# A decoder layer with a routed feed-forward network: three sorted groups of 2, 3 and 2 batches instead of four of 1, 2, 2 and 2

## The chip, the cores and the metric

The kernel runs on one core of a Trainium2 chip. The metric is the device time of one execution in microseconds (us). A core has a matrix engine (PE; its weight loads are listed as PEld), a vector engine (DVE), a scalar engine (ACT), a general engine (POOL), and a queue, SP, that does no arithmetic here and starts most of the transfers. Each engine takes its instructions in the order in which they are written, and waits at a semaphore until another engine or a transfer has raised it.

## The reference

The input `x` has 8 batches of 256 tokens of width 128. Three blocks follow one another, each with a residual and a layer norm: attention with selected keys, retention against a context, and a feed-forward network with 8 experts, of which each token takes the two with the highest gate. The last one is what the change touches:

```
logits = x_flat @ gate_w.T;  probs = softmax(logits)
topk_probs, topk_idx = top_k(probs, 2)
hidden = relu(einsum('th,ehf->tef', x_flat, w1) + b1)      # 8 experts, 128 -> 512
all_out = einsum('tef,efh->teh', hidden, w2) + b2          # 512 -> 128
y = sum(take_along_axis(all_out, topk_idx) * topk_probs)
x = layernorm(x + y)
```

The reference works out all experts for all tokens. The kernel does so for the last batch alone; for the other seven it sorts tokens by expert.

## The kernel before

**Steps and slots.** The whole kernel is one pipeline, written by the function `program` that every engine walks through. Step n (n from -2 to 8) has 20 slots. In slot s of step n, each engine gets its instructions of four stages: attention's preparation for batch n+1 (stage a), attention's 16 query tiles of batch n (stage b, one in each of slots 0 to 15), retention and the second norm of batch n-1 (stage c), and the router (stage d), whose gates and counts for batch n-1 stand in slots 16 to 19. Step 7 has no stage a, step 8 neither a nor b.

**Sorted groups.** Batches 0 to 6 are taken in groups (`GROUPS`). A group's tokens, each twice, once for each chosen expert, are laid out in DRAM so that each stretch of 128 rows belongs to one expert. Since the number of tokens of an expert is known only at run time, a group of b batches needs as many tiles as the worst case: `most_tiles` = (2·256·b + 8·127) // 128, which is 11 for one batch, 15 for two and 19 for three. All of them are computed, empty or not. A group goes through this:

- `tile_list(g)`, in slot 2 of the step that is two behind its last batch. DVE works out each token's row (`slot`) and each tile's expert (`lrow`), in a chain of small operations with four for each batch. POOL then scatters the tokens of each batch with four indirect transfers (L780). SP waits for `lrow`, starts the weights of three tiles, waits for the scatter, and loads the first rows.
- `tile(g, k, q)`: the tiles, one in each tile slot of the plan. In tile k's slot PE does the second product of tile k (L1202), the turning of tile k+2's rows, and the first product of tile k+1 (L1185); ACT does four rectifications (L1467), DVE two copies out of PSUM (L1855, L1862). Two slots (k = -2 and -1) start a group and one (k = number of tiles) only stores. SP starts the expert weights of tile k+3 (578 KB), the rows of tile k+4 and the store of tile k-1. Up to the last group, `tile` shares the bank `bR` with retention and router; in the last group (`g == ALONE`), which runs in step 8, it uses the banks that attention has left.
- For each batch: `collect` (G; POOL gathers its rows with four indirect transfers, L768), `summed` (S; POOL, three operations), `means` (M; DVE and ACT, statistics) and `normed` (N; root on DVE, normalising on POOL in L808, and SP, which waits for POOL and stores the batch, L628). The last group's and batch 7's stand behind the last slot, with batch 7's eight experts (`dense`).

**The plan.** `plan` fills the free tile slots in order: in steps 2 to 7 the nine `TILE_SLOTS`, in step 8 the 22 `END_SLOTS`. A group begins in slot 6 or later of the step of its list. This is what it gives before, T for tiles computed:

```
step 2: list of batch 0 in slot 2; 3 tiles of group 0 (slots 13, 15, 17)
step 3: 8 tiles of group 0; G0 in slot 19
step 4: S0, M0, N0 (slots 0, 7, 8); list of 1, 2; 3 tiles of group 1
step 5: 9 tiles of group 1
step 6: 3 tiles of group 1 (0, 1, 2); list of 3, 4; G1 S1 G2 S2 M1 N1 M2; 3 tiles of group 2
step 7: N2 in slot 0; 9 tiles of group 2
step 8: 3 tiles of group 2; list of 5, 6; G3 S3 G4 M3 S4 N3 M4 N4 in slots 5 to 18; 15 tiles of group 3
behind: batch 7 with all 8 experts; G S M N of batches 5 and 6
```

## Time and profile before

| | |
|---|---|
| median of 3 runs | 766.42 us (762.03 to 773.82) |
| the profiled execution | 757.35 us, of which its span is 755.5 us |
| PE busy | 644.0 us, 85% of the span |
| DVE busy | 473.1 us, 63% |
| ACT busy | 369.5 us, 49% |
| POOL busy | 274.7 us, 36% |
| granted clock of PE, mean | 0.868 of full |
| weights `wt` | 64 loads of 578 KB, median 4.1 us from issue to landing |

How to read it: busy time is the sum of an engine's instructions, and a busy PE can still be slower than it might be, since its clock changes between half and full. The span is shown in 40 slices, with the clock in each. What a step costs is read from windows: a step begins here where ACT's first exponential of that batch begins (51.5, 114.4, 180.7, 253.9, 326.6, 407.0, 481.6 and 562.1 us for steps 0 to 7), and step 8 where PE starts the tile of its slot 0 (639.5 us).

### The profile page before, as it was taken

What the parts mean: (1) busy time and instruction counts of PE and PEld (TensorE: products, weight loads), DVE (VectorE), ACT (ScalarE), POOL (GpSimd) and SP (SyncE); (2) the same over time, 40 slices, a digit from 0 to 9 for tenths busy, and PEclk for the clock granted to TensorE, in tenths of its full rate; (3) what the DMA queues carried; (4) which work ended last, traced back from release to release, by engine and by line L of the source; (5) the groups of instructions that cost most, each with busy time, mean ns of one, the idle gap of its engine ahead of it and who ended that gap; (6) DMA issues with size and microseconds to landing.
All of it is one profiled execution on the core that took longest, in us unless ns stands there. A gap on an engine that the chain in (4) does not pass through costs nothing.

```text
span 755.5 us, 18822 instructions
## 1 busy us (share of the span) xinstructions
PE 644.0 (85%) x6549; PEld 495.8 (66%) x6549; DVE 473.1 (63%) x1733; ACT 369.5 (49%) x1271; POOL 274.7 (36%) x451
## 2 busy tenths in 40 slices
PE   5469988997999899988998999889977997567794
PEld 4245664675577677755686777757766776457794
DVE  1618647876985797578766975687744674314334
ACT  4335445453565476544554766355533643234352
POOL 0345602911840163139701540179622001342053
PEclk9857598897799999965899999968986998669998
DMA  4080030020306330303044416040523222248760
GB/s 150 1 299 2 2 106 1 2 107 1 124 3 204 108 97 19 111 16 129 9 170 127 116 41 195 23 144 17 172 86 101 87 82 64 87 138 267 227 214 26
DMA packets 43413, 73.23 MB, mean 97 GB/s; under 512 B 7664, under 2 KB 31544, under 8 KB 42168
## 3 DMA queue, kind: packets, MB, share of 16 engines
q1 hardware_dynamic: 41528, 68.36, 28.7%
q0 software_dynamic: 1792, 3.67, 1.5%
q8 instruction: 53, 0.87, 0.5%
q14 instruction: 40, 0.33, 0.1%
HBM read 61.69 MB, written 10.32 MB: 95 GB/s over the span
## 4 chain that ended last, share of the span: by engine, by line
PE 44%; issue 10%; POOL 9%; DVE 8%; ACT 3%; DMA 1%; POOLq 0%; DVEq 0%
PE bM L830 6%; PE bG L975 5%; PE bH L1185 5%; PE bR L1202 4%; PE bM L1018 3%; PE bS L994 3%; PE bM L1023 2%; POOL sorted_tokens L780 2%; PE bR L1107 2%; PE bW L1247 2%; PE bS L991 2%; PE bC L830 2%; PE bC L1124 2%; PE bW L1202 1%; PE bC L1075 1%
## 5 line engine op out<-in xcount | busy, mean ns | idle before, releaser
L1385 ACT ACTIVATE pp<-pp,nmx 128x224 f32<-128x224 f32 x96 | 46.4, 483 | 79.5 <-DVE nmx L1662 78.1
L1668 DVE TENSOR_TENSOR gs<-bG,rank_t 96x512 f32<-96x512 f32 x96 | 65.5, 682 | 18.5 <-PE bG L975 18.5
L1467 ACT ACTIVATE ht<-bH,wt 128x128 f32<-128x128 f32 x192 | 54.7, 369 | 39.1 <-PE bH L1185 39.1
L1397 ACT COPY pts<-bM 128x256 f32<-128x256 f32 x96 | 35.4, 369 | 63.0 <-PE bM L830 62.7
L1731 DVE TENSOR_TENSOR sm<-bC,cst 128x512 f32<-128x512 f32 x64 | 43.6, 681 | 34.0 <-PE bC L1124 33.6
L1202 PE MATMUL bR<-wt,ht 128*128 128x128 f32 x328 | 51.1, 305 | 15.8 <-DVE taken L1808 13.3
L726 POOL TENSOR_TENSOR r<-x,cst 128x256 f32<-128x256 f32 x8 | 5.8, 724 | 153.7 <-DVE x L1695 153.7
L975 PE MATMUL bG<-oh,kspl 128*96 128x512 f32 x160 | 61.3, 467 | 0.0
L1202 PEld LDWEIGHTS bR<-wt,ht 128*128 128x128 f32 x328 | 46.9, 215 | 21.2 <-issue 15.1
L1185 PE MATMUL bH<-xt,wt 128*128 128x128 f32 x384 | 56.6, 295 | 4.1 <-DVE xt L1855 2.0
L1650 DVE TENSOR_SCALAR ppn<-pp,rls 128x224 f32<-128x224 f32 (+1 forms) x128 | 49.8, 389 | 14.1 <-DVE rls L1647 0.5
L830 PE MATMUL bM<-cst,ppn 128*128 128x128 f32 (+1 forms) x224 | 56.2, 323 | 0.9 <-DVE ppn L1650 0.9
L1185 PEld LDWEIGHTS bH<-xt,wt 128*128 128x128 f32 x384 | 52.5, 210 | 5.8 <-DVE xt L1855 2.7
L1662 DVE CUSTOM_DVE_ANT_0 pp<-bS,cst 128x224 f32<-128x224 f32 x96 | 36.5, 380 | 29.1 <-PE bS L994 29.1
L1018 PE MATMUL bM<-pts,ckw 96*32 96x64 f32 x512 | 52.6, 293 | 0.3 <-ACT ots L1405 0.3
L1124 PE MATMUL bC<-qV,kS 128*128 128x512 f32 x64 | 37.0, 578 | 13.1 <-DVE sm L1731 10.6
L994 PE MATMUL bS<-gs,qall 96*32 96x128 f32 x768 | 44.7, 308 | 1.0 <-DVE gs L1668 0.2
L780 POOL DMA_INDIRECT sorted_tokens<-x,slot x28 | 29.9, 1068 | 42.7 <-DVE slot L1837 27.5
L1018 PEld LDWEIGHTS bM<-pts,ckw 96*32 96x32 f32 x512 | 19.5, 113 | 39.2 <-issue 38.3
L1023 PEld LDWEIGHTS bM<-pts,vgs 128*32 128x32 f32 x1536 | 44.2, 121 | 0.0
L830 PE MATMUL bM<-cst,gs 32*128 32x32 f32 x384 | 44.0, 236 | 0.0
L1023 PE MATMUL bM<-pts,vgs 128*32 128x16 f32 x1536 | 43.4, 198 | 0.0
(288 smaller groups left out, 1595.9 us busy)
## 6 DMA issues: line engine op xcount, KB each, us to landing
wt<-in_experts SPq DMA_DIRECT2D x64, 578.0 KB, 4.1
sidx<-far_slots SPq DMA_DIRECT2D x8, 1536.0 KB, 7.0
xs<-sorted_tokens SPq DMA_DIRECT2D x56, 64.0 KB, 3.7
expert_rows<-ot SPq DMA_DIRECT2D x56, 64.0 KB, 3.5
sorted_tokens<-acc SPq DMA_DIRECT2D x11, 256.0 KB, 7.8
cst<-shape_constants SPq DMA_DIRECT2D x1, 1603.5 KB, 6.3
xn<-in_x SPq DMA_DIRECT2D x8, 128.0 KB, 4.9
xr<-in_x SPq DMA_DIRECT2D x8, 128.0 KB, 3.2
```

Source lines behind the costliest of these rows:

```text
L830: return MM(dst, src, ident[lo:lo + n, lo:lo + n], is_transpose=True, start=True, stop=True)
L975: last = MM(w[0:96, :], table, oh[:, pair % 2, kt, SLOTS * (tile % 2):SLOTS * (tile % 2) + SLOTS], start=(n == 0), stop=(n == len(products ...
L994: last = MM(bS[32 * c:32 * c + 32, o + 96:o + SW], qall[0:96, p, 128 * tile + 32 * c:128 * tile + 32 * c + 32], gs[:, g % 2, 128 * c:128 * ...
L1018: last = MM(bM[32 * j:32 * j + 32, WEIGHED:WEIGHED + 64], near, pts[0:96, 0:128].rearrange("p (q a b) -> p b a q", a=4, b=2)[:, j, :, :], ...
L1023: last = MM(bM[32 * j:32 * j + 32, WEIGHED:WEIGHED + 64].rearrange("p (a q) -> p a q", a=4)[:, :, 4 * c:4 * c + 4], vgs[:, g % 2, 32 * c:3 ...
L1124: full(MM(w[:, :], kS[:, t, g, :], qV[:, g, :, :], start=True, stop=True))
L1185: last = MM(w[:, 128 * f:128 * f + 128], wt[:, t % NW, 128 * f:128 * f + 128], xt[:, t % 2, :], start=True, stop=True)
L1202: last = MM(w[:, 0:128], ht[:, t % 2, f, :], wt[:, t % NW, W2_AT + 128 * f:W2_AT + 128 * f + 128], start=(f == 0), stop=(f == 3))
L1385: AC(pp[:, s % 2, 0:w], bS[:, 0:w] if s < T0 else pp[:, s % 2, :], ACT.Exp, scale=1.0 if s < T0 else -1.0, bias=nmx[:, s % 2:s % 2 + 1], a ...
L1467: last = AC(ht[:, t % 2, f, :], w[:, 128 * f:128 * f + 128], ACT.Relu, bias=wt[:, t % NW, FF + f:FF + f + 1])
L1650: TS(ppn[:, t % 2, 0:w], pp[:, t % 2, 0:w], rls[:, t % 2:t % 2 + 1], None, ALU.mult).then_inc(s_nrm.sem, 1)
L1668: TT(gs[:, g % 2, :].rearrange("p (t j) -> p t j", j=FAR), bG[0:96, :].rearrange("p (t j) -> p t j", j=FAR), rank_t[:, :].rearrange("p (o ...
```

## The change

The groups are (0, 1), (2, 3, 4) and (5, 6), with 15, 19 and 15 tiles: 49 instead of 56. There are three lists instead of four. Steps 6 and 7 get eleven tile slots instead of nine (`FULL_SLOTS`), and step 2 none. `plan` puts sums, statistics and normalising at other distances behind the last tile: in step 8 three slots apart for each batch instead of four, and five slots behind the gather instead of eight. Since three batches wait for their list at a time, `hm` and `place` hold three batches (`PART_OF`); `tile_row` and `row_start` are stored once and broadcast. The new plan:

```
step 2: no tile, no list
step 3: list of 0, 1 in slot 2; 3 tiles of group 0 (slots 13, 15, 17)
step 4: 9 tiles of group 0
step 5: 3 tiles of group 0 (0, 2, 4); G0 7, S0 10, G1 11, M0 12, N0 13, S1 14
step 6: list of 2, 3, 4 in slot 2; M1 4, N1 5; 5 tiles of group 1 (10, 11, 13, 15, 17)
step 7: 11 tiles of group 1 (0, 2, 4, 5, 8, 9, 10, 11, 13, 15, 17)
step 8: 3 tiles of group 1; list of 5, 6; G2 5, G3 8, S2 8, M2 10, G4 11, S3 11, N2 11,
        M3 13, N3 14, S4 14, M4 16, N4 17; 15 tiles of group 2
```

```diff
-GROUPS = tuple((b, most_tiles(b)) for b in ((0,), (1, 2), (3, 4), (5, 6)))
+GROUPS = tuple((b, most_tiles(b)) for b in ((0, 1), (2, 3, 4), (5, 6)))
 DENSE = NB - 1
+PART_OF = [n - next(b for b, _ in GROUPS if n in b)[0] for n in range(DENSE)] + [2]
-ALONE = 3
+ALONE = 2
-MOST = 16
+MOST = 20
 TILE_SLOTS = (0, 2, 4, 5, 8, 10, 13, 15, 17)
+FULL_SLOTS = (0, 2, 4, 5, 8, 9, 10, 11, 13, 15, 17)
 LIST_SLOT, FIRST_SLOT = 2, 6
-MEAN_LATE = 8
...
-    at, free = {}, [(step, s) for step in range(2, NB) for s in TILE_SLOTS] + [(NB, s) for s in END_SLOTS]
+    at, free = {}, [(step, s) for step in range(3, NB) for s in (TILE_SLOTS if step < 6 else FULL_SLOTS)] + [(NB, s) for s in END_SLOTS]
...
-            s += 2 + 4 * (n - GROUPS[g][0][0])
-            for table, late in ((gather, 0), (first, 3), (second, MEAN_LATE), (third, MEAN_LATE + 1)):
-                table[step + (s + late) // NS, (s + late) % NS] = n
+            s += 2 + (4 if step < NB else 3) * (n - GROUPS[g][0][0])
+            mean = NS * step + s + 5
+            if step < NB and not 4 <= mean % NS < 16:
+                mean += 8
+            for table, here in ((gather, NS * step + s), (first, NS * step + s + 3), (second, mean), (third, mean + 1)):
+                table[here // NS, here % NS] = n
...
-        hm, hot = sb("hm", [128, 2, 2, 2, NE]), sb("hot", [128, 2, NE], BF16)
+        hm, hot = sb("hm", [128, 3, 2, 2, NE]), sb("hot", [128, 2, NE], BF16)
-        taken, place = sb("taken", [128, NE]), sb("place", [128, 2, 2, NE])
+        taken, place = sb("taken", [128, NE]), sb("place", [128, 3, 2, NE])
```

The two places that the prediction speaks of, as the instructions stand in order. First SP in step 8, in the last group's tiles: `wt` are a tile's weights, `xs` its rows, `expert_rows` the store of a tile, `out` that of a whole batch, and `lrow` the reading of four tiles' expert numbers. Before, from the weights of tile 10 on:

```order
L581 DMA wt<-in_experts 128x1156
L572 DMA xs<-sorted_tokens3 128x128
L595 DMA expert_rows3<-ot 128x128
L581 ISA
L581 DMA wt<-in_experts 128x1156
L572 DMA xs<-sorted_tokens3 128x128
L595 DMA expert_rows3<-ot 128x128
L628 DMA out<-acc 128x2x128
L194 TENSOR_LOAD lrow
L194 ISA x8
L581 ISA
```

In the change, from the weights of tile 7 on (four lines further down in the file):

```order
L585 DMA wt<-in_experts 128x1156
L576 DMA xs<-sorted_tokens2 128x128
L599 DMA expert_rows2<-ot 128x128
L632 DMA out<-acc 128x2x128
L198 TENSOR_LOAD lrow
L198 ISA x8
L585 ISA
L585 DMA wt<-in_experts 128x1156
L576 DMA xs<-sorted_tokens2 128x128
L599 DMA expert_rows2<-ot 128x128
```

The first store of a batch in the last group's tiles stood between the weights of tiles 11 and 12, and now stands between those of tiles 7 and 8; a second one stands where the first was.

Then PE in step 7, in slots 8 to 10: L991/L995 to L975/L979 are attention's scores and gather, L1202/L1206 and L1185/L1189 a tile's two products, the others attention's transposes and weighing. Before, from slot 8's tile on:

```order
L1202 MATMUL bR<-wt,ht 128x128 x4
L830 MATMUL bR<-cst,xs 128x128
L1018 MATMUL bM<-pts,ckw 32x64 x2
L1023 MATMUL bM<-pts,vgs 32x4x4 x8
L830 MATMUL bM<-cst,gs 128x32 x4
L830 MATMUL bM<-cst,ppn 128x128 x2
L1124 MATMUL bC<-qV,kS 128x512
L1185 MATMUL bH<-xt,wt 128x128 x4
L991 MATMUL bS<-kd,qall 128x96
L994 MATMUL bS<-gs,qall 32x128 x4
L975 MATMUL bG<-oh,kspl 96x512 x2
L1018 MATMUL bM<-pts,ckw 32x64 x2
```

In the change:

```order
L1206 MATMUL bR<-wt,ht 128x128 x4
L834 MATMUL bR<-cst,xs 128x128
L1022 MATMUL bM<-pts,ckw 32x64 x2
L1027 MATMUL bM<-pts,vgs 32x4x4 x8
L834 MATMUL bM<-cst,gs 128x32 x4
L834 MATMUL bM<-cst,ppn 128x128 x2
L1128 MATMUL bC<-qV,kS 128x512
L1189 MATMUL bH<-xt,wt 128x128 x4
L995 MATMUL bS<-kd,qall 128x96
L998 MATMUL bS<-gs,qall 32x128 x4
L979 MATMUL bG<-oh,kspl 96x512 x2
L1206 MATMUL bR<-wt,ht 128x128 x4
```

In slot 9, where attention went on with L1018 directly, a second product (and behind it the rest of a tile) has come in; the same holds for slot 11.

## Rows read from the trace of the kernel before

**Rows 1.** Windows, steps 1 to 8: us; busy PE, PEld, DVE, ACT, POOL; clock; DMA; GB/s.

```profile
114.40:180.70 66.30, 58.40 (x670) 41.30 (x670) 50.92 (x181) 35.39 (x124) 24.95 (x45) 0.90 0.09 32
180.70:253.90 73.20, 65.92 (x724) 48.66 (x724) 54.85 (x199) 39.09 (x140) 27.31 (x49) 0.88 0.31 99
253.90:326.60 72.70, 70.15 (x804) 55.44 (x804) 53.40 (x195) 43.08 (x152) 26.22 (x49) 0.96 0.25 75
326.60:407.00 80.40, 70.71 (x724) 51.69 (x724) 58.30 (x211) 40.14 (x141) 37.19 (x58) 0.80 0.29 95
407.00:481.60 74.60, 70.24 (x824) 55.69 (x824) 54.06 (x199) 45.29 (x159) 22.32 (x45) 1.00 0.34 104
481.60:562.10 80.50, 72.81 (x769) 56.06 (x770) 59.40 (x220) 41.18 (x148) 47.81 (x68) 0.86 0.31 99
562.10:639.50 77.40, 67.44 (x756) 53.81 (x754) 44.35 (x152) 35.03 (x132) 8.08 (x15) 0.87 0.28 81
639.50:755.50 116.00, 83.28 (x579) 74.31 (x579) 40.48 (x161) 40.84 (x125) 41.76 (x48) 0.84 0.50 156
```

**Rows 2.** Windows: slots 7 to 14 of steps 1 and 5, slots 15 to 19 of step 1.

```profile
142.70:168.90 26.20, 24.95 (x357) 17.82 (x357) 20.93 (x69) 14.48 (x49) 10.23 (x19) 1.00 0.22 78
436.40:466.60 30.20, 30.18 (x396) 23.98 (x395) 21.23 (x75) 17.96 (x62) 7.39 (x17) 1.00 0.39 125
168.90:180.70 11.80, 9.01 (x117) 7.60 (x109) 6.97 (x34) 4.74 (x17) 0.44 (x1) 1.00 0.01 2
```

**Rows 3.** Windows: slots 0 to 3 of steps 7 and 5.

```profile
562.10:581.10 19.00, 13.23 (x69) 10.60 (x68) 8.88 (x27) 7.15 (x28) 7.01 (x10) 0.59 0.35 98
407.00:423.00 16.00, 14.60 (x115) 10.93 (x116) 13.28 (x44) 11.99 (x46) 1.99 (x4) 1.00 0.32 91
```

**Rows 4.** Timeline of PE: one tile in step 3 (start us, us, engine, line).

```profile
269.15 1.05 PE L1202 MATMUL bR<-wt,ht 128*128 128x128 f32 x8
...
270.24 0.41 PE L1018 MATMUL bM<-pts,ckw 96*32 96x64 f32 x4
...
271.09 1.06 PE L1185 MATMUL bH<-xt,wt 128*128 128x128 f32 x8
271.90 0.48 PE L1124 MATMUL bC<-qV,kS 128*128 128x512 f32 x1
```

**Rows 5.** Timeline of DVE: first and last operation of the list in step 4.

```profile
334.15 0.18 DVE L1818 TENSOR_TENSOR flag<-taken,cst 128x32 f32<-128x32 f32 x1
...
337.33 0.16 DVE L1845 TENSOR_SCALAR lrow<-owner 1x16 int32<-1x16 f32 x1
```

**Rows 6.** Timeline of POOL: step 6's scatter, first and last of eight.

```profile
492.58 1.09 POOL L780 DMA_INDIRECT sorted_tokens<-x,slot  x1 [8.90 <-DVE slot L1837]
...
502.47 0.96 POOL L780 DMA_INDIRECT sorted_tokens<-x,slot  x1 [0.32 <-issue]
```

**Rows 7.** Timeline of POOL in step 8: G3 (first, fourth), S3 (first, last), N3.

```profile
669.57 0.98 POOL L768 DMA_INDIRECT gb<-expert_rows,slot  x1 [6.68 <-DMA expert_rows<-ot]
...
673.37 0.94 POOL L768 DMA_INDIRECT gb<-expert_rows,slot  x1 [0.31 <-issue]
675.93 1.04 POOL L797 TENSOR_TENSOR gb<-gb,v 128x512 f32<-128x512 f32 x1 [1.62 <-DMA gb<-expert_rows,slot]
...
677.86 0.72 POOL L799 TENSOR_TENSOR acc<-acc,x 128x256 f32<-128x256 f32 x1
...
698.65 1.57 POOL L808 TENSOR_SCALAR acc<-acc,fmv,fln 128x128 f32<-128x128 f32 x2 [8.60 <-DVE fln L1688]
```

**Rows 8.** Timeline of SP and PE in step 8: N3's store, weights, first products.

```profile
693.10 1.06 PE L1185 MATMUL bG<-xt,wt 128*128 128x128 f32 x8
...
700.25 0.39 SPq L628 DMA_DIRECT2D out<-acc  x1
702.18 0.34 SPq L581 DMA_DIRECT2D wt<-in_experts  x1
...
706.17 1.75 PE L1185 MATMUL bG<-xt,wt 128*128 128x128 f32 x8 [2.47 <-issue]
```

More of the change, by code:

```diff
@@ L151, in constants @@
     c["before"] = (p[:, None] < p[None, :]) * 1.0
-    c["tile_row"] = np.tile(np.repeat(np.arange(MOST) * 1.0, NE), (128, 1))
+    c["tile_row"] = np.tile(np.arange(MOST) * 1.0, (128, 1))
     c["nothing"] = np.zeros((128, NE))
     for size in sorted({len(b) for b, _ in GROUPS}):
-        c[f"row_start{size}"] = np.tile(np.arange(size * L // 128) * 128.0, (128, NE))
+        c[f"row_start{size}"] = np.tile(np.arange(size * L // 128) * 128.0, (128, 1))
     return c
@@ L1769, in router @@
                 for r in range(2):
-                    k = od.did(TT(hm[:, i.par, r, :, :], C("expert_no").rearrange("p (o e) -> p o e", o=1).broadcast_to([128, 2, NE]),
+                    k = od.did(TT(hm[:, PART_OF[i.n], r, :, :], C("expert_no").rearrange("p (o e) -> p o e", o=1).broadcast_to([128, 2, NE]),
                                   f8[:, :, r:r + 1].broadcast_to([128, 2, NE]), ALU.is_equal))
                 od.wait(k)
-                TT(hot[:, :, :], hm[:, i.par, 0, :, :], hm[:, i.par, 1, :, :], ALU.add).then_inc(r_m.sem, 1)
+                TT(hot[:, :, :], hm[:, PART_OF[i.n], 0, :, :], hm[:, PART_OF[i.n], 1, :, :], ALU.add).then_inc(r_m.sem, 1)
             oe = Own(dve, own_ve)
@@ L1779, in gates @@
                 for r in range(2):
-                    k = oe.did(TT(hm[:, i.par, r, :, :], C("expert_no").rearrange("p (o e) -> p o e", o=1).broadcast_to([128, 2, NE]),
+                    k = oe.did(TT(hm[:, PART_OF[i.n], r, :, :], C("expert_no").rearrange("p (o e) -> p o e", o=1).broadcast_to([128, 2, NE]),
                                   f8[:, :, r:r + 1].broadcast_to([128, 2, NE]), ALU.is_equal))
@@ L1783, in gates @@
                 for t in range(2):
-                    k = oe.did(TS(gg[:, t, :], hm[:, i.par, 0, t, :], v8[:, i.n, t, 0:1], None, ALU.mult))
+                    k = oe.did(TS(gg[:, t, :], hm[:, PART_OF[i.n], 0, t, :], v8[:, i.n, t, 0:1], None, ALU.mult))
                 oe.wait(k)
                 for t in range(2):
-                    last = STT(gg[:, t, :], hm[:, i.par, 1, t, :], v8[:, i.n, t, 1:2], gg[:, t, :], ALU.mult, ALU.add)
+                    last = STT(gg[:, t, :], hm[:, PART_OF[i.n], 1, t, :], v8[:, i.n, t, 1:2], gg[:, t, :], ALU.mult, ALU.add)
                 last.then_inc(r_gate.sem, 1)
@@ L1818, in tile_list @@
                 k = ol.did(TT(each(flag[:, 0:n]), taken[:, :].rearrange("p (e o) -> p e o", o=1).broadcast_to([128, NE, n // NE]),
-                              each(C(f"row_start{len(batches)}")), ALU.is_gt))
+                              C(f"row_start{len(batches)}").rearrange("p (o r) -> p o r", o=1).broadcast_to([128, NE, n // NE]), ALU.is_gt))
                 ol.wait(k)
@@ L1828, in tile_list @@
                     base = row0[:, :].rearrange("p (o e) -> p o e", o=1).broadcast_to([128, 2, NE])
-                    k = os_.did(TT(place[:, b % 2, :, :], place[:, b % 2, :, :], base, ALU.add))
+                    k = os_.did(TT(place[:, PART_OF[b], :, :], place[:, PART_OF[b], :, :], base, ALU.add))
                     os_.wait(k)
                     k = os_.did(TT(qq[:, :, :].rearrange("p (r t) e -> p r (t e)", r=2),
-                                   hm[:, b % 2, :, :, :].rearrange("p r t e -> p r (t e)"),
-                                   place[:, b % 2, :, :].rearrange("p (o t) e -> p o (t e)", o=1).broadcast_to([128, 2, 2 * NE]), ALU.mult))
+                                   hm[:, PART_OF[b], :, :, :].rearrange("p r t e -> p r (t e)"),
+                                   place[:, PART_OF[b], :, :].rearrange("p (o t) e -> p o (t e)", o=1).broadcast_to([128, 2, 2 * NE]), ALU.mult))
                     os_.wait(k)
@@ L1840, in tile_list @@
                 k = ol.did(TT(past[:, :, :], ends_row.broadcast_to([1, MOST, NE]),
-                              C("tile_row", 1).rearrange("p (t e) -> p t e", e=NE), ALU.is_le))
+                              C("tile_row", 1).rearrange("p (t o) -> p t o", o=1).broadcast_to([1, MOST, NE]), ALU.is_le))
                 ol.wait(k)
```

2 lines of the change are left out of this document (1 added, 1 removed).

## The prediction

> **What bounds the kernel now.** I read the busy times first: PE 85%, DVE 63%, so PE is the candidate, but with room. Then windows step by step [rows 1]. Steps with a list cost more than steps with tiles: step 5 with 9 tiles and no list takes 74.6 us, step 4 with 3 tiles, a list of two batches and one combination takes 80.4. Step 1, with neither, takes 66.3. So a tile in a step without a list is cheap, (74.6 − 66.3) / 9 = 0.9 us, and a list is dear. Third, windows inside steps [rows 2]: slots 7 to 14 take 26.2 us in step 1, where PE is busy 24.95, and 30.2 in step 5, where three tiles fall in them and PE is busy 30.18. There PE is full and a tile costs (30.2 − 26.2) / 3 = 1.3 us, since it first fills PE's gaps. Without gaps it would cost what PE gives it: in the timeline the second product and the turning go from 269.15 to 270.24 and the first product from 271.09 to 271.90, 1.9 us together [rows 4]. Seven tiles at that full price are 13.3 us; that is the most that the title of the change can be worth in PE work.
>
> The lists are dear for two reasons. DVE's chain, from 334.15 to 337.49, holds DVE for 3.3 us in a stretch in which it is full of other work [rows 5], and PE goes slower for lack of work: mean clock 0.80 in step 4 against 1.00 in step 5 [rows 1].
>
> **The change, step by step.** I take each new step as a step of the trace that has the same load. Up to 180.7 us nothing changes but some columns of constants, at no cost.
>
> Step 2 loses its list and three tiles and becomes step 1: 66.3 for 73.2, −6.9 (from −8 to −5: the clock of step 1 was 0.90).
>
> Step 3 had 8 tiles and no list, 72.7; it gets a list of two batches and three tiles. That is the load of step 2 (73.2, a list of one) with four more small DVE operations, 0.2 us each by the operations in [rows 5], 0.9 with their waits, so 74.1 at least. Step 4, which also has three tiles and a list of two, took 80.4, but it combined batch 0 as well and ran at a clock of 0.80. I take 75.5, nearer to step 2 since nothing is combined here: +2.8 (+1.4 to +7.7).
>
> Step 4 had 80.4; it gets nine tiles and no list, which is step 5: 74.6, −5.8 (−7.7, if it is step 3, to −5).
>
> Step 5 had 74.6. It keeps three tiles in slots 0 to 4 and loses six. Its slots 0 to 6 stay at 29.4 (407.0 to 436.4); slots 7 to 14 become those of step 1, 26.2, and slots 15 to 19 too, 11.8 [rows 2]: 67.4. It gets the combination of batch 0 and half of that of batch 1; step 4 is 7.2 longer than step 2 through one combination, one more batch in the list and a lower clock, and I give the combination 1.5 of it. 68.9, −5.7 (−7.2 to 0, if it were all 7.2).
>
> Step 6 had 80.5 with 6 tiles, a list of two and most of two combinations. It gets 5 tiles, the list of three and M1, N1. By step 4: 80.4 + 0.9 + two more tiles at 1.3 = 83.9. By step 2: 73.2 + 2 × 0.9 + 2.6 = 77.6. I take 81.5, a little above the middle, since M1 and N1 stand among DVE's busiest slots: +1.0 (−2.9 to +3.4). POOL's scatter becomes longer, 12 indirect transfers for 8. Eight took from 492.58 to 503.43 [rows 6], so four add 5.4 us. Behind them on POOL stands attention's preparation for the next batch, which slots 7 and 10 want. SP waits for the scatter too, but the first tile's rows are wanted only in slot 8. I cost both at nothing because step 6 loses G1, G2, S1 and S2; if that cover is too small, up to 2 us of PE waiting for POOL come on top.
>
> Step 7 had 77.4. Its slots 0 to 3 took 19.0 us at a clock of 0.59, against 16.0 at 1.00 for the same slots of step 5, which even have stage a in them [rows 3]: batch 2's normalising, in slot 0 of step 7, and the statistics before it hold the queues there. They leave, −3.0. Two tiles come, in slots 9 and 11. In step 7 PE has no gaps to fill from slot 7 on, so I take 1.9 each [rows 4], +3.8. Sum +0.8 (−2.5 with 1.3 a tile and 2 us of clock more, to +3.8).
>
> Step 8 has as many tiles as before, but combines three batches for two, and closer together. G2 begins where G3 began, 669.6, as the same store precedes it. Four gathers take 5.0 with their gaps (669.57 to 674.31, and 0.3), the sum 2.65 (675.93 to 678.58) [rows 7]. In POOL's new order: G2 to 674.6, G3 to 679.6, S2 to 682.3. M2 then needs DVE for about 1.2 us, an estimate from five operations of 0.2 and a little more for their width [rows 5]; G4 waits for it: 683.5 to 688.5, S3 to 691.2, N2 1.6 more [rows 7], 692.8. SP waits for exactly that to store batch 2, and behind it in SP's queue stand the expert numbers and the weights of tile 8. In the trace N3's store at 700.25 is followed by weights at 702.18, and the first product that uses them starts at 706.17 after PE had waited 2.47 [rows 8]: 1.93 and 3.99 us. So tile 8's first product can start at 692.8 + 1.9 + 4.0 = 698.7. It starts at 693.10 now [rows 8]. **+5.6**, and nothing else on PE can fill it, because PE takes its instructions in order. The bounds: 0 if the slots before it run late enough by themselves, +10 if the clock falls behind the wait.
>
> Sum: −6.9 + 2.8 − 5.8 − 5.7 + 1.0 + 0.8 + 5.6 = **−8.2 us**. The profiled execution took 757.35 us (span 755.5), so its counterpart should take 749.1. The runs have a median of 766.42 and spread by 11.8; the profiled one lies 9 below the median. I carry the difference over: 766.42 − 8.2 = **758.2**.
>
> Removed POOL and DVE work of the fourth list does not stand in the sum by itself; the step windows have it. The weight loads saved, 7 of 578 KB, cost nothing now, as the share of DMA in steps 3 to 7 is 0.25 to 0.34 [rows 1].
>
> **The clock, row against rule.** Slots 7 to 14 of step 1 have no tile and ran at a clock of 1.00, PE busy 24.95 of 26.2 [rows 2], so I let steps 2 and 5 keep their clock without tiles. The Trainium skill ("TensorE: Matmul & The Clock Gate", section "Why this matters for your kernels") says that gaps between bursts of matmuls drop the clock to half, and taking tiles out widens the gaps. The trace agrees where gaps are wide: 0.59 at the start of step 7, with PE busy 13.23 of 19.0 [rows 3]. By the row the sum is −8.2; by the rule, applied to every tile-free stretch, it would be the second rival's sum.
>
> **Rivals.** A, *PE gives back the full price*: every tile taken out counts 1.9 us, 13.3 together, the list's DVE chain, once less, about 1.7 net of the longer ones, the stall at the start of step 7 3.0, and SP's wait for N2 is hidden since POOL is faster than I think. −18.0: 739.4 in profile, 748.4 as a median. For it: PE is busy 30.18 of 30.2 where tiles are. Against: steps with 8 or 9 more tiles than step 1 are only 6.4 and 8.3 us longer [rows 1].
>
> B, *the clock*, which ends slower: tile-free steps 2 and 5 and the head of step 3 are run at the clock of step 4. Price: the 7.2 us between steps 4 and 2 for each of steps 2 and 5, −8.2 + 14.4 = +6.2, 772.6. It decides when their clock is under about 0.85. For it: steps 2 and 4 with three tiles had 0.88 and 0.80, step 5 with nine 1.00. Against: [rows 2].
>
> C, *SP's queue*, twice: N3 in step 8 blocks tile 12 a second time by as much, with half clock behind both waits, and the scatter of three holds POOL in step 6 (2 us). −8.2 + 5.6 + 2 = −0.6, 765.8. Against: N3 now has its turn after tile 8 as before, so its wait shifts with the tiles.
>
> **Chances.** Forecast 0.50, A 0.26, B 0.10, C 0.14. The range takes in A and the lower bounds of steps 5 and 8 in part, and B's sum: 743 to 772. About 2%, 15.3 us, is what a measurement can tell from no change here. Faster by more than that needs the median under 751.1: A with most of its share, 0.19, and the forecast's low end, with several steps at their lower bounds, 0.08: 0.27. Slower by more needs +15: B and C together, 0.03. Within 2%: 0.70.
>
> **What would show it.** In the changed profile: step 2 near 66 and step 5 near 69 us with clocks over 0.9; step 4 near 74.6; steps 3 and 6 with clocks near 0.8; in step 8 a wait of PE of some 5 us before the first product of tile 8, with SP storing a batch just before; no dear slot 0 in step 7. I am wrong if PE has no such wait (then A), if step 2 or 5 stays at over 72 us (B), or if a second wait of over 4 us stands before tile 12 (C).

## The result, and the profile after

Measured beside each other in 20 runs each, the changed kernel took **770.39 us** (761.42 to 775.53) and the kernel before 761.97 us (760.11 to 773.82). The ratio is 1.0077, 95% interval [1.0046, 1.0107]: slower by 0.8%, which is less than the 2% that the prediction counts as a change, but more than the measurement's own uncertainty. Two later comparisons on other chips gave 1.0035 [0.999, 1.008] and 1.0067 [1.0036, 1.0099]. The forecast was 8.2 us faster, and that is wrong: the median of 770.4 lies in the range of 743 to 772, but on the other side of no change. An execution over 1.5% above the fastest of its kernel in the same set is counted as slow and left out of the ratios; such are the executions behind the trace that the prediction was read from and behind five of those below (on chip B the changed kernel unchanged and the later normalising, on chip D both repairs, on chip E the kernel before and the parted transfers).

The profiled execution took 768.8 us (span 767.0). The windows of its steps 1 to 8 answer to [rows 1]:

```profile
113.20:177.40 64.20, 55.81 (x670) 39.37 (x670) 50.66 (x181) 35.06 (x123) 25.10 (x45) 0.95 0.10 33
177.40:242.70 65.30, 57.36 (x670) 40.54 (x670) 50.95 (x182) 35.19 (x123) 24.79 (x45) 0.92 0.11 32
242.70:319.80 77.10, 68.06 (x724) 50.04 (x724) 55.31 (x204) 39.45 (x139) 32.80 (x53) 0.84 0.30 97
319.80:395.80 76.00, 71.70 (x824) 57.17 (x824) 54.40 (x199) 45.30 (x159) 22.30 (x45) 0.98 0.35 104
395.80:474.90 79.10, 69.54 (x719) 51.77 (x719) 54.42 (x193) 37.11 (x133) 40.38 (x61) 0.84 0.11 36
474.90:563.00 88.10, 72.53 (x750) 53.91 (x750) 59.53 (x219) 41.00 (x147) 38.27 (x59) 0.81 0.32 105
563.00:639.60 76.60, 70.27 (x794) 56.42 (x794) 45.58 (x153) 37.19 (x139) 6.75 (x13) 0.92 0.33 96
639.60:767.00 127.40, 85.28 (x579) 75.67 (x579) 44.81 (x169) 40.83 (x127) 49.57 (x57) 0.83 0.47 145
```

Read the first column against the terms of the sum. Step 2 fell as forecast (65.3 us, 66.3 forecast), steps 3, 4 and 7 are within 2 us. Three steps are far off: step 5 was to take 68.9 us at a high clock and took 79.1 at 0.84; step 6 took 88.1 for 81.5; step 8 grew by 11.4 for 5.6.

**Step 5.** Its slots 0 to 6, 7 to 14 and 15 to 19 were forecast at 29.4, 26.2 and 11.8 us, plus 1.5 for the combinations:

```profile
395.80:422.90 27.10, 24.91 (x260) 18.04 (x260) 23.61 (x84) 18.01 (x68) 12.39 (x23) 1.00 0.03 9
422.90:455.00 32.10, 29.72 (x348) 20.88 (x348) 22.36 (x76) 14.45 (x51) 21.55 (x28) 0.84 0.21 68
455.00:474.90 19.90, 14.92 (x120) 12.84 (x115) 8.45 (x34) 4.65 (x16) 6.44 (x12) 0.61 0.07 20
```

The first part is better than forecast. The miss is in the other two, where the forecast used slots of step 1 that had run at a clock of 1.00: 5.9 us in slots 7 to 14, at 0.84, and 8.1 in slots 15 to 19, at 0.61. The timeline of POOL in the second half of the step:

```profile
453.19 1.64 POOL L812 TENSOR_SCALAR acc<-acc,fmv,fln 128x128 f32<-128x128 f32 x2 [7.74 <-DVE fln L1692]
454.80 0.73 POOL L730 TENSOR_TENSOR r<-cn,cst 128x256 f32<-128x256 f32 x1
...
456.55 0.72 POOL L735 TENSOR_TENSOR rkn<-r 128x256 f32<-128x256 f32 x1
```

and the timeline of PE at the same time:

```profile
455.67 0.44 PE L834 MATMUL bM<-cst,ppn 128*128 128x128 f32 x2
460.10 1.09 PE L834 MATMUL bC<-cst,rks 128*128 128x128 f32 x4 [4.00 <-DVE rks L1572]
```

POOL stood 7.74 us for the normalising of batch 0 (L812), and the rotation of the retention keys (L730 to L735) was queued behind it. DVE makes rks, the rotated keys, from its result, and PE waited 4.00 us for rks. This wait belongs to slots 15 to 19; it says nothing about slots 7 to 14. The order of POOL's queue was changed by the table that puts batch 0's normalising into slot 13, and I had costed only the combination's own work.

**Step 8.** The timeline of SP, with the first store and what follows it, and the second store:

```profile
692.63 0.39 SPq L632 DMA_DIRECT2D out<-acc  x1
694.57 0.34 SPq L585 DMA_DIRECT2D wt<-in_experts  x1
...
706.59 0.39 SPq L632 DMA_DIRECT2D out<-acc  x1
708.52 0.34 SPq L585 DMA_DIRECT2D wt<-in_experts  x1
```

and the timeline of PE, its two longest waits in that stretch:

```profile
698.53 2.05 PE L1189 MATMUL bH<-xt,wt 128*128 128x128 f32 x8 [3.61 <-issue]
...
712.55 2.05 PE L1189 MATMUL bH<-xt,wt 128*128 128x128 f32 x8 [3.44 <-issue]
```

This is the forecast wait, 5.9 us after the store as the sum had it (1.9 + 4.0): tile 8's first product was forecast for 698.7 and started at 698.53 (step 8 begins at 639.6 here and at 639.5 in the trace of the kernel before, so the two can be compared). The second wait stands before tile 12, where the kernel before had one of 2.47 us [rows 8]; it is now 3.44. So one wait is new, and the old one has grown by 1.0. The product after each takes 2.05 us where the one between takes 1.06: the granted clock is 0.50 from 698.5 to 701.5 and 0.52 from 712.5 to 715.5, and 1.00 from 704 to 706.

**Step 6.** The timeline of DVE:

```profile
493.00 0.66 DVE L1735 TENSOR_TENSOR sm<-bC,cst 128x512 f32<-128x512 f32 x1
498.69 0.39 DVE L1666 CUSTOM_DVE_ANT_0 pp<-bS,cst 128x224 f32<-128x224 f32 x1 [5.03 <-remote]
```

and of PE:

```profile
492.69 0.66 PE L998 MATMUL bS<-gs,qall 96*32 96x128 f32 x8
...
495.40 0.77 PE L1128 MATMUL bC<-qV,kS 128*128 128x512 f32 x1
499.15 0.74 PE L995 MATMUL bS<-kd,qall 128*128 128x96 f32 x2 [2.98 <-DVE nmx L1666]
```

DVE waits for the scores that PE wrote in L998. Their recorded end is 493.35, DVE goes on at 498.69, 5.3 us later, and PE waits for DVE in turn. I call this a **late signal**. POOL issues its twelve scatters from 484.4 to 499.9, 0.3 us apart. I count a signal as late where DVE or ACT waits for a matmul and goes on over 1 us after its recorded end. The changed kernel's trace then has seven places or stretches of them (around 260, 444, 494, 661, 677, 689 and 743 us), and the trace of the kernel before has none.

Of what the prediction named as signs: step 2 near 66, step 4 near 74.6 (76.0) and the wait before tile 8 (3.61 us, some 5 forecast) are there. The dear slot 0 of step 7 is gone only in part, since slots 0 to 3 there (563.0 to 579.0) had a clock of 0.72. One sign of the rivals is there as well, step 5 over 72 (B). The sign of C, a second wait of over 4 us before tile 12, is not: it is 3.44.

### The profile page after: what moved, and what is told of

Its sections match the earlier page's. It is cut to its first block and busy times, and to the rows that moved or that the text cites. A ratio compares the mean times of both kernels' runs of the same rounds, so it can differ in the third digit from the quotient of the medians.

```text
span 767.0 us, 18441 instructions
## 1 busy us (share of the span) xinstructions
PE 632.2 (82%) x6430; PEld 482.0 (63%) x6430; DVE 473.4 (62%) x1713; ACT 360.4 (47%) x1243; POOL 278.5 (36%) x451
## 5 line engine op out<-in xcount | busy, mean ns | idle before, releaser
L730 POOL TENSOR_TENSOR r<-x,cst 128x256 f32<-128x256 f32 x8 | 5.8, 726 | 183.5 <-DVE x L1699 183.5
L1471 ACT ACTIVATE ht<-bH,wt 128x128 f32<-128x128 f32 x168 | 48.0, 369 | 49.5 <-PE bH L1189 44.5
L1189 PE MATMUL bH<-xt,wt 128*128 128x128 f32 x336 | 51.3, 301 | 11.4 <-issue 7.8
L979 PE MATMUL bG<-oh,kspl 128*96 128x512 f32 x160 | 59.4, 454 | 0.0
L1189 PEld LDWEIGHTS bH<-xt,wt 128*128 128x128 f32 x336 | 47.3, 214 | 13.2 <-issue 8.2
L1206 PE MATMUL bR<-wt,ht 128*128 128x128 f32 x272 | 41.1, 299 | 13.7 <-DVE taken L1812 11.1
L1206 PEld LDWEIGHTS bR<-wt,ht 128*128 128x128 f32 x272 | 37.1, 207 | 18.8 <-issue 12.4
L995 PE MATMUL bS<-kd,qall 128*128 128x96 f32 x192 | 39.6, 291 | 7.7 <-DVE nmx L1666 7.6
L998 PE MATMUL bS<-gs,qall 96*32 96x128 f32 x768 | 43.9, 303 | 2.4 <-DVE gs L1672 0.2
L1022 PEld LDWEIGHTS bM<-pts,ckw 96*32 96x32 f32 x512 | 19.4, 112 | 40.1 <-issue 39.1
```

Of the source, the lines that this page charges most:

```text
L979: last = MM(w[0:96, :], table, oh[:, pair % 2, kt, SLOTS * (tile % 2):SLOTS * (tile % 2) + SLOTS], start=(n == 0), stop=(n == len(products ...
L998: last = MM(bS[32 * c:32 * c + 32, o + 96:o + SW], qall[0:96, p, 128 * tile + 32 * c:128 * tile + 32 * c + 32], gs[:, g % 2, 128 * c:128 * ...
L1022: last = MM(bM[32 * j:32 * j + 32, WEIGHED:WEIGHED + 64], near, pts[0:96, 0:128].rearrange("p (q a b) -> p b a q", a=4, b=2)[:, j, :, :], ...
L1189: last = MM(w[:, 128 * f:128 * f + 128], wt[:, t % NW, 128 * f:128 * f + 128], xt[:, t % 2, :], start=True, stop=True)
L1206: last = MM(w[:, 0:128], ht[:, t % 2, f, :], wt[:, t % NW, W2_AT + 128 * f:W2_AT + 128 * f + 128], start=(f == 0), stop=(f == 3))
L1471: last = AC(ht[:, t % 2, f, :], w[:, 128 * f:128 * f + 128], ACT.Relu, bias=wt[:, t % NW, FF + f:FF + f + 1])
```

## The experiments

Eighteen runs followed, of fourteen kernels, on five further chips (here B to F; the first comparison is A). Ratios are always against the kernel before, run in turns on the same chip. Each run left one trace, so where the text sets windows of two runs side by side, it compares one execution with one. "Tail" is the time from the last exponential of attention in step 7 to the end: 130.8 us in the first trace of the kernel before, 142.2 in that of the changed kernel.

### Chip B: the changed kernel again, one repair each, and the tiles alone

The changed kernel unchanged:

> The changed kernel once more, nothing edited. Its first profile has six places (at 260, 442, 493, 660, 676 and 741 us) where PE's semaphores rise 1.3 to 5.9 us after the recorded end of the matmul that raises them, with DVE and ACT waiting; the profile of before has none. Theory P (these late signals are a part of the change's cost): they come again at the same places, and the time is again 767 to 772. Rival (an accident of one execution): they stand elsewhere or are gone, and a profile without them has a span near 755 to 760. In either case a PE wait of some 3.5 us before the first product of tile 8 of the last group, and one of some 4 us for the split keys at the end of step 5.

Measured: 1.0035 [0.999, 1.008]. Its trace has no late signal anywhere, so they are no fixed part of the change. Its span is 765.7 all the same and not near 755 to 760: steps 0 to 2 took 210.0 us, 20 more than in the first trace, at clocks of 0.72, 0.79 and 0.82. Step 6 is 80.7 (81.5 forecast) and the tail 136.0, 5.2 more than before (5.6 forecast). Before tile 8 PE waited 4.91, before tile 12 3.53, and in step 5 1.95 for rks. At the place of step 6 shown above, DVE's timeline reads:

```profile
506.83 0.66 DVE L1735 TENSOR_TENSOR sm<-bC,cst 128x512 f32<-128x512 f32 x1
507.42 0.37 DVE L1666 CUSTOM_DVE_ANT_0 pp<-bS,cst 128x224 f32<-128x224 f32 x1
```

No gap, with the same twelve scatters running (498.19 to 514.4). So the scatters alone do not make the signals late; something that differs between chips or executions has to be there too.

Batch 0's normalising two slots later:

```
-            for table, here in (..., (third, mean + 1)):
+            for table, here in (..., (third, mean + (3 if n == 0 else 1))):
```

> The changed kernel with batch 0's normalising moved from slot 13 to slot 15 of step 5, so that on POOL the rotation of retention's keys (slot 14) stands ahead of it and not behind it. Theory W (order in the queues costs what was not foreseen): PE's wait of 4.0 us for the split keys at 460 us goes, step 5 falls from 79 to about 75 us, the time by 4 us. Rival C (the half clock of the tile-free half of step 5 sets its length): the wait goes but step 5 stays within 1.5 us, since what PE does behind it is as slow as before.

Measured: 0.999 [0.9929, 1.0051]; step 5 71.0 us at a clock of 0.93, 3 under the changed kernel beside it. PE's wait for rks is gone. Slots 15 to 19 take 11.8 us at a clock of 1.00, as the prediction had them, while slots 7 to 14 stay at 32.2 at 0.84. The gain in time is not clear of noise.

SP's stores of batches 2 to 4 two slots later in step 8:

```
+STORE_AT = {(step, s + 2 if step == NB else s): n for (step, s), n in NORM_AT.items()}
...
+                    if stored and (step, s) in STORE_AT:
+                        stored(STORE_AT[step, s])
```

> The changed kernel with the stores of batches 2, 3 and 4 issued by SP two slots later in step 8 than they are normalised; POOL, DVE, ACT and PE keep their order. Theory W (SP's queue blocks the weights of tiles 8 and 12): PE's waits of 3.6 and 3.4 us before the first products of these tiles go, and the time falls by 5 to 7 us. Rival: the sums of batch 4, which need batch 2's store to have landed, and through them the statistics come later and hold DVE: no gain, or under 2 us.

Measured: 0.9918 [0.9875, 0.996], 1.2% under the changed kernel; the intervals of the two do not meet. The tail is 125.1. PE's waits for SP's weights in step 8, 4.91 and 3.53 in the changed kernel beside it, are now 0.36, 0.83 and 1.08:

```profile
689.40 1.13 PE L1196 MATMUL bH<-xt,wt 128*128 128x128 f32 x8 [0.36 <-issue]
...
692.36 1.13 PE L1196 MATMUL bG<-xt,wt 128*128 128x128 f32 x8 [0.83 <-issue]
...
697.91 1.13 PE L1196 MATMUL bG<-xt,wt 128*128 128x128 f32 x8 [1.08 <-issue]
```

The kernel before with seven tiles fewer, its groups kept and the slots left empty; the rows of those tiles are left out:

```
+LEFT_OUT = (1, 2, 2, 2)
+GROUPS = tuple((b, most_tiles(b) - m) for b, m in zip(((0,), (1, 2), (3, 4), (5, 6)), LEFT_OUT))
```

> The kernel before with 10, 13, 13 and 13 tiles in its four groups, 49 for 56; the slots of the seven left-out tiles stay empty, and every list, gather, sum and normalising keeps its slot. It leaves out the last one or two tiles of each group. It prices the seven tiles alone. By the forecast's cheap price (0.9 to 1.3 us a tile) the time falls by 6 to 9 us, by the full price (1.9) by 13 us. If PE's clock falls where the tiles are missing, by under 4 us.

Measured: 0.9769 [0.9673, 0.9866], 17 us for seven tiles. By the interval it is 10 to 25 us, so the 13.3 that I had as the most is not ruled out. The tail is 119.7, 11.1 less than in the first trace of the kernel before, and it loses four of the seven tiles. The regrouping takes no tile out of step 8: there are the second products of 19.4 tiles behind the last exponential before and after, 15.4 here.

### Chip C: is it the stores, and what is a tile worth in step 8?

The kernel before with late stores (the same table, bounded to slot 19):

> The kernel before, with SP's stores of the combined batches in step 8 two slots later, nothing else. Theory (SP's queue is dear only where its wait for the normalised batch comes out above the work behind it, and the kernel before had one such wait of 2.47 us, ahead of tile 12): the gain is small, 2 to 4 us, ratio 0.995 to 0.998, and step 8 falls from 116.0 to some 113. The regrouping with the same edit then is ahead of it or level, by 746.5 for the changed kernel with late stores against 752 to 754 here. Rival (late stores help either kernel alike, since what they relieve is the end of the kernel and not the two waits that the regrouping made): ratio 0.99 or below, and the regrouping itself is worth nothing.

Measured: 0.9996 [0.9958, 1.0033]. A gain of the late stores in the kernel before is not to be seen; the interval leaves room for 0.4%. So what they gain on chip B is for the most part a loss that the regrouping had made.

Both repairs:

> The changed kernel with both repairs: batch 0 normalised two slots later in step 5, so that it stands behind the retention's key rotation on POOL, and SP's stores in step 8 two slots later. Theory (two separate losses, one in step 5 and one in step 8): step 5 at 71 or less, step 8 near 110; the late normalising alone measured 0.999 and the late stores 0.992 against the kernel before, the changed kernel 1.0035, so the two together give about 0.988, some 746 us. Rival (the clock takes back in the next steps what step 5 gives): level with late stores alone, 0.992.

Measured: 0.994 [0.9912, 0.9969]; step 5 71.0 at 0.93. Here, too, the signals are late: step 6 87.2, tail 131.4.

Both repairs, and the middle group's 19 tiles ended in step 7:

```
-FULL_SLOTS = (0, 2, 4, 5, 8, 9, 10, 11, 13, 15, 17)
+FULL_SLOTS = (0, 2, 4, 5, 8, 9, 10, 11, 12, 13, 14, 15, 16, 17)
...
+    late = ((2, ((7, 17), (8, 0), (8, 4), (8, 5))), (3, ((8, 3), (8, 6), (8, 8), (8, 9))), ...)
```

> The changed kernel with both repairs and with tiles moved out of step 8: step 7 takes all that is left of the middle group, twelve tiles, and step 8 only the last group's fifteen, with the gathers of batches 2 to 4 a few slots earlier. The number of tiles stays at 49. Theory (a tile is cheap in steps 3 to 7, at most 1.9 us, and costs over 3 us in step 8, where the kernel with seven empty tile slots fewer lost 10.9 us for three tiles): step 8 falls by some 10 us against the one with both repairs, step 7 and 6 grow by 2 to 6 us together, ratio 0.977 to 0.985. Rival (the price in step 8 is the last group's chain from its list to its last gather, which does not get shorter by this): level with both repairs, step 7 longer by what step 8 gives.

Measured: 1.0031 [0.9987, 1.0075], 0.9% behind both repairs. Step 6 grew by 8.7 for three tiles, the tail stayed at 131.5, although four tiles had left it and the last group's rows were loaded some 6 us sooner. In the tail the time went here, in PE's timeline:

```profile
667.56 0.47 PE L847 MATMUL bS<-cst,xs 128*128 128x128 f32 x1 [1.47 <-issue]
676.09 0.79 PE L1141 MATMUL bC<-qV,kS 128*128 128x512 f32 x1 [8.06 <-issue]
```

In these 8 us POOL issued five indirect transfers, gathers of batches 3 and 4, and ACT went on 7.9 us after the recorded end of the matmul that it waited for: a late signal again. The time is level, as the rival had it, but its reason, the chain of the last group, is not what shows. The edit moves the sums and normalisings of batches 2 to 4 too, so it is no test of a tile's place alone.

The kernel before with three tiles fewer in its last group (`GROUPS = GROUPS[:3] + ((GROUPS[3][0], GROUPS[3][1] - 3),)`); their rows are left out:

> The kernel before with twelve tiles instead of fifteen for the last group of two batches; what would have stood in the last three tiles is left out. It gives the price of a tile in step 8 by itself. Theory (3.3 to 3.6 us each there, since in the last step nothing else is left that fills PE while a tile's chain runs): 10 to 11 us less, ratio 0.985 to 0.987. Rival (a tile costs PE's own 1.9 us as elsewhere, and the seven tiles less gained their 17 us otherwise): 4 to 6 us less, ratio 0.992 to 0.995.

Measured: 0.9925 [0.9884, 0.9967], 5.7 us, 1.9 a tile (0.8 to 3.0 by the interval). The rival holds, my 3.3 to 3.6 was wrong; I had counted three tiles for four in the kernel with 49. The price read in [rows 4] fits step 8.

### Chip D: more PE work in the steps without tiles

> The changed kernel with both repairs once more, as the base for the two kernels with added PE work on the same chip. Theory (the two losses are the wait in step 5 and SP's two waits in step 8): 0.99 against the kernel before, as in the first measurement (0.994 [0.991, 0.997]); the same again if the repairs don't depend on the chip.

Measured: 0.9985 [0.9941, 1.003]. That is less of a gain than on chip C (0.994 [0.9912, 0.9969]), but the two intervals overlap, so that the repairs depend on the chip is not shown. In its trace PE's wait for rks is gone, and yet slots 15 to 19 of step 5 take 16.2 us at a clock of 0.50: here the clock fell 7 us before them.

> The changed kernel with the late stores alone once more, beside the one with both repairs. Theory (normalising batch 0 two slots later has a gain of its own, 3 to 6 us in step 5, through a wait of 4 us that goes and the clock behind it): 0.4 to 0.8% behind both repairs. Rival (it has none, step 5's length is the clock's luck): level with both repairs within 0.3%.

Measured: 0.9986 [0.9946, 1.0026], level with both repairs: the rival holds. What the earlier normalising costs is too small for these measurements.

A product without a reader in every slot, or every second one, of the steps without tiles:

```
+                    if fill and step >= 0 and (step < 3 or (step == 5 and s >= 7)):
+                        fill()
...
+            def fill():
+                MM(bH[:, 0:256], ident, wq_all[:, 0:256], start=True, stop=True)
```

> Both repairs, and in every slot of the steps that have no tile (steps 0, 1, 2 and slots 7 to 19 of step 5) one more product on PE, of 128 by 256 elements, whose result nobody reads: 73 products, about 0.3 us each at full clock, 22 us of PE work. Theory (the clock falls in tile-free stretches for lack of PE work, half clock for 12 to 24 us in a step, and more work keeps it up, as the tiles of step 4 did in all traces, 0.98 to 1.00): clocks of steps 0, 1, 2 and 5 over 0.95, and the kernel within 5 us of the one with both repairs, or faster. Rival (PE is full there, and the clock falls for other reasons): clocks as before, 0.72 to 0.95, and 10 to 20 us slower.

> The same added product in every second slot only, 36 of them, 11 us of PE work. Theory (half the dose keeps part of the clock): between both repairs and the full dose in clock, and level with or faster than both repairs. Rival: half of the loss of the full dose, 5 to 10 us slower.

Measured: 1.0058 [1.0022, 1.0094] in every slot, 0.9942 [0.99, 0.9983] in every second. Clocks of steps 0, 1, 2, 5: late stores alone 0.88, 0.90, 0.85, 0.84; full dose 0.97, 0.95, 0.95, 0.83; half dose 0.99, 0.90, 0.95, 0.85. With more work on PE the clock is higher in two or three of the steps 0 to 2. It gains nearly nothing there: the three steps take 193.7 us with half the dose, 198.0 with the full one and 194.7 with late stores alone. In time the full dose is some 0.7% behind both repairs, with intervals that just overlap; half the dose is not told apart from them. In step 5 the clock does not rise: in both traces it is at half from slot 13 or so nearly to the end of the step.

### Chip E: late signals in both kernels, and the scatter in step 6

> The changed kernel once more, as the base for this chip. Theory (where PE's signals come late beside POOL's indirect transfers the regrouping is slower by more, since step 6 has twelve of them in a row): 1.005 to 1.01 against the kernel before, if its trace shows such late signals, step 6 near 88; 1.000 to 1.004 and step 6 near 81, if it shows none.

> The kernel before, for its trace on this chip. Theory (POOL's indirect transfers make the signals late in either kernel, and it is the chip or the execution that decides whether they do): late signals here if the changed kernel has them, beside POOL's lists and gathers, steps 3 and 4 together some 6 us longer than in the first trace (72.7 and 80.4), step 6 hardly (80.5). Rival (only the regrouping has them): none in this trace.

Measured: 1.0067 [1.0036, 1.0099] for the changed kernel, which has the late signals. The kernel before has them as well, at seven places, each of them beside indirect transfers of POOL, and its steps 3 and 4 are 6.6 us longer than in the first trace, as expected. The rival is out: the regrouping did not make them. But it has more of them: the waits behind them add up to 20 us in the trace of the kernel before and to 39 in that of the changed one, with 56 indirect transfers in either. How much of this the time feels is not known.

The kernel before was here also run against itself: 0.9958 [0.991, 1.0007], where 1 is right. A difference of 0.4% in a ratio should therefore not be believed by itself.

The changed kernel's trace in the worst stretch of late signals, by the window:

```profile
491.90:505.00 13.10, 5.55 (x28) 3.11 (x27) 5.87 (x21) 3.77 (x17) 10.33 (x15) 0.58 0.59 186
```

PE is busy 5.55 of 13.1 us. The scatter cut to batch 2's four transfers; batches 3 and 4 are left out:

```
-                for n in GROUPS[g][0]:
+                for n in GROUPS[g][0][:1] if g == 1 else GROUPS[g][0]:
```

> The changed kernel with the scatter of step 6 cut from twelve indirect transfers to four; the rows of batches 3 and 4 are left out. Theory (PE stands still there because its signals come late while POOL issues indirect transfers): if this chip has late signals, the stretch of them in step 6 becomes a third as long and step 6 falls by 5 to 9 us, to near 81; without late signals by 2 us at most. Rival (the step is long through its tiles and the list of three on DVE): step 6 falls by 2 us at most in either case.

Measured: 0.9993 [0.9953, 1.0032], 0.7% or 6 us under the changed kernel. The stretch of late signals shrank from 13.1 us (491.9 to 505.0) to 3.6 (492.8 to 496.4), while the others stayed. Step 6 itself fell only from 88.9 to 87.1, its clock from 0.81 to 0.75. So the transfers are shown to be a condition of the lateness there, one that does not suffice by itself (chip B). Whether it is POOL's issuing or the transfers' own traffic is not parted, and in which step the time is saved is not shown.

The twelve transfers in three parts, in slots 2, 4 and 6 (`SENT_AT = (2, 4, 6)`, a call `sent(g, part)` that issues one batch's four):

> The changed kernel with the twelve transfers of step 6 issued four at a time in slots 2, 4 and 6, so that attention's preparation on POOL stands between them. Theory (late signals and POOL's block of 15 us both hurt because the twelve are in a row): step 6 falls by 3 to 6 us where signals come late, 1 to 2 us where not; ratio 0.3 to 0.7% under the changed kernel. Rival (the lateness is by the number of transfers, not by their being in a row): three short stalls for one long one, and level.

Measured: 1.0056 [1.0022, 1.009], level with the changed kernel (1.0067). The rival forecast the time, but not for the right reason. In the trace of the parted transfers two short late signals are left in step 6, 500.9 to 503.8 and 513.4 to 514.5, in place of the stretch of 13.1 us: parting them helped against the lateness. In its place stands a new wait of PE:

```profile
531.73 0.47 PE L840 MATMUL bR<-cst,xs 128*128 128x128 f32 x1 [5.79 <-DMA xs<-sorted_tokens]
```

These are the rows of the group's first tile. SP loads them when the last of the twelve transfers has landed, and POOL issued the last four only at 523.1 to 528.6. In the changed kernel beside it, the scatter ended at 503.9 and the same product waited 0.47 us, for DVE.

### Chip F: the tiles spread over steps 4 and 5

```
+SPREAD = {4: (0, 4, 8, 10, 13, 17), 5: (0, 2, 5, 8, 10, 13, 15)}
...
-            if step < NB and not 4 <= mean % NS < 16:
+            if step < NB and not 2 <= mean % NS < 16:
```

> The changed kernel with late stores, and group 0's tiles spread out: six tiles in step 4 and seven in step 5 (slots 0 to 15) instead of nine and four, so that step 5 is not without tiles from slot 7 on. The combinations of batches 0 and 1 move to slots 17 of step 5 to 7 of step 6. Theory (step 5's clock of 0.79 to 0.85 comes from its tile-free half, and the wait for batch 0's normalising with it): clock of step 5 at 0.95 or more and step 5 at 71 to 74, though it has three tiles more; step 4 at 71 to 73; step 6 longer by the combinations, 1 to 4 us; in all 0.3 to 0.8% under the base. Rival (the clock of step 5 does not hang on tiles): 0.80 to 0.85 again, step 5 at 80 or more, and level with the base or slower.

> The changed kernel with late stores, as the base for spread tiles on this chip. Theory (late stores take away the two waits behind SP's queue, some 8 to 10 us of step 8 in every trace so far, against 8.4 to 5.2 that the regrouping added there): 0.992 to 0.999 against the kernel before, step 8 with its last attention 125 to 133 us.

Steps 4 and 5 with spread tiles:

```profile
323.50:396.80 73.30, 67.07 (x773) 52.17 (x773) 53.26 (x193) 41.79 (x147) 25.01 (x45) 0.95 0.29 88
396.80:469.90 73.10, 68.91 (x770) 54.21 (x770) 54.62 (x192) 40.18 (x144) 31.32 (x52) 0.92 0.18 53
```

The base has 74.6 at 1.00 and 79.2 at 0.84 for the two. Step 5 is 6 us shorter with three tiles more, at a clock of 0.92 (I had expected 0.95), and step 6 is no longer than the base's (91.9 for 91.5). Slots 7 to 14, which now have tiles, run at a clock of 1.00 in 29.1 us, against 32.3 at 0.84 in the base. So step 5 hangs on where the tiles and the combinations stand; the edit moves both, and the two are not parted. In time it is unclear: 0.9964 [0.9923, 1.0006] against 0.9959 [0.9914, 1.0004], medians 757.1 and 761.2.

No version that computes everything is faster than the kernel before by 2%. Late stores had 0.9918, 0.9986 and 0.9959 on three chips and both repairs 0.994 and 0.9985 on two, so 0.4 to 0.5% on average. The kernel before differed from itself by 0.4% on chip E.

## Why the prediction was wrong, step by step

The two traces of chip E are the fairest pair, since both have late signals and nearly the same steps 0 and 1 (61 and 66.2 us in both); each of the two executions lies within 1.2 us of its kernel's median there. It is one execution of each, and a step with the same instructions differs by 2 us and more between executions. Differences, changed kernel less kernel before:

| step | before | changed | difference | forecast | miss |
|---|---|---|---|---|---|
| 2 | 73.3 | 67.8 | −5.5 | −6.9 | +1.4 |
| 3 | 76.5 | 77.6 | +1.1 | +2.8 | −1.7 |
| 4 | 83.2 | 74.6 | −8.6 | −5.8 | −2.8 |
| 5 | 75.9 | 79.3 | +3.4 | −5.7 | **+9.1** |
| 6 | 83.8 | 88.9 | +5.1 | +1.0 | **+4.1** |
| 7 | 75.4 | 75.1 | −0.3 | +0.8 | −1.1 |
| 8 | 119.1 | 127.7 | +8.6 | +5.6 | +3.0 |
| sum | | | +3.8 | −8.2 | +12.0 |

**Steps 2, 3, 4 and 7** came out by their mechanism: a step costs what a step with the same load costs, and the list is the dear part. Together they are 4.2 us better than forecast.

**Step 5 is the step that failed.** I pieced it together from slots of step 1 and of the old step 5, both at a clock of 1.00. It ran at 0.77 to 0.84 and took 74.1 to 80.7 us in all eight traces whose step 5 has its queue order and tiles as the change made them, for a forecast of 68.9. The term that failed is the pair of windows from step 1. Slots 7 to 14 took 29.1 to 34.5 us in these traces and not 26.2, at 0.77 to 0.90; slots 15 to 19 took 17.8 to 19.9 at 0.50 to 0.61 and not 11.8 at 1.00. Rival B named this step and a price of 7.2 us, and came near (the miss is 9.1); step 2 kept its gain. For slots 15 to 19 the order on POOL is a part: with the normalising behind the rotation PE's wait for rks is gone in all four traces, and these slots took 11.7 and 11.8 us at 1.00 in two of them, as forecast. In the other two they took 16.2 and 16.3 at 0.50; there the clock had fallen before them. For slots 7 to 14 nothing was found that mends them but the kernel with spread tiles (1.00). Added products did not help the step (0.83, 0.85), which speaks against a simple lack of PE work. So what lowers the clock there, the missing tiles or the combinations that came in, is open.

**Step 6** was sized at 81.5 and is right on the chip without late signals (80.7). Where they occur, it took 86.8 us or more. I had read in [rows 6] how long POOL is held, and costed what waits for POOL. That matmuls' signals can come late beside transfers on POOL was in no row of the trace that I had, and no rival held it.

**Step 8** has the forecast wait. Counted from the last exponential of attention, tile 8's first product starts 5.3 us later than before in the first pair of traces and 6.0 later on chip E, for a forecast of 5.6. On chip B it starts only 2.2 later, and that the whole step grew by 5.2 there is in part luck. Rival C did not come true: from tile 8 to tile 12 it takes 13.0 and 14.0 us in the two traces of the kernel before and 14.0 to 14.4 in the three of the changed one, and on chip E PE waits 3.38 us before tile 12 in the kernel before and 3.39 in the changed one. What goes beyond the forecast lies for the most part behind the last tile, 1.9 us on chip E and 4.3 in the first pair, but 0.4 on chip B, which has no late signals.

**Rival A** failed: the change takes its seven tiles out of steps 2 to 7 and none out of step 8, where three tiles less gave 1.9 us each. That tiles in steps 2 to 7 are cheaper, as the prediction has it, is argued from windows; no run priced them there, and the kernel with 49 tiles speaks against it, with 2.5 us for each of its seven (1.4 to 3.5 by the interval).

**The carry-over to the median** rested on one trace of the kernel before without late signals, from an execution 9 us under the median that the prediction had. On chip E its counterpart with them took 767.2 us of span for 755.5. The 20 runs of the first comparison have nothing under 760.11, and the set of the profiled execution (757.35) has one of 746.2 or less, 1.5% below it. Runs as short as that were seen on chip B alone (745.5 to 768.0). So trace and median were probably not of one state of things, and adding −8.2 to the median assumed that they were. The record does not name the chip of either.

## What to carry to other kernels

Taking work out of a kernel pays by the place: ask for every tile that goes which step it leaves, and what its going does to the clock there and to the order of each in-order queue. A window taken from another step brings its clock along; if the load around it differs, give it the lower clock as a second price. When a table moves an instruction that waits (a store on SP, a normalising on POOL), write down what now stands behind it; issuing the stores two slots later cost nothing here and gained up to 1.2%. And look at more than one trace of the kernel before if its runs spread: what makes them differ may hit the changed kernel harder.

## What the runs showed of the hardware

**Late signals beside indirect transfers.** In the traces of chips C to F, and in that of the changed kernel on A, other engines go on 1 to 8 us after the recorded end of the matmul that they wait for. Every one of these places has indirect transfers of POOL beside it, one to eleven; with eight of twelve taken away the stretch in step 6 shrank from 13.1 to 3.6 us. In all four traces of chip B there was not one, with the same transfers, and none in the first trace of the kernel before. On chip B the kernel before was 6 to 13 us faster (755.6 against 762.0 to 768.2 us). The Trainium skill ("Perfetto Trace Analysis", section "Per-engine timelines") says that the profiler estimates the end of a matmul, from the instruction's size, and does not observe it. So the traces cannot tell a matmul that ended late from a signal that travelled late, and which it was stays open, as does what sets chip B apart.

**The clock differs between executions of the same instructions.** Steps 0, 1 and 2 of the changed kernel, 190.1 us at clocks of 0.88, 0.95 and 0.92 in its first trace, took 210.0 at 0.72, 0.79 and 0.82 in the next: 20 us, 2.6% of the span. Step 1, which every version but those with added products has alike, took 66.2 or 66.3 us at 0.90 in thirteen of eighteen traces, 64.2 at 0.95 in one, and 71.9 or 72.0 at 0.79 in four. The Trainium skill ("TensorE: Matmul & The Clock Gate", section "What's actually happening") puts the penalty of the clock's ramp, at the start of a kernel, at under 1% of a typical span. Here the clock also falls again later: in the trace of the changed kernel to half from 459.4 to 483.3 us and from 654.0 to 674.4, among others.
